# Fused AdaLN, linear attention and mixture of experts on one core: fewer TensorE signals, longer GELU and weight rings

## What is computed

```python
h = _layernorm(x, axis=-1) * (1 + ca) + sa
x = x + ga * _L0_attn_ref(h, ...)      # 8 heads of 16
h = _layernorm(x, axis=-1) * (1 + cb) + sb
x = x + gb * _L0_ffn_ref(h, ...)       # 8 experts of 256, 2 per token
```

```python
num = jnp.einsum('bshd,bhde->bshe', q, kv) * scale + vsum[:, None, :, :]
den = jnp.einsum('bshd,bhd->bsh', q, ksum) * scale + seq_len
o = num / den[..., None] + lepe_conv(v, lepe_w, lepe_b)   # 5 taps along the tokens
o = o.reshape(Bb, Ss, H * DV) * o_gate
return o @ Wo.T
```

```python
h = jax.nn.gelu(jnp.einsum('bsd,edh->besh', x, W1) + b1[None, :, None, :], approximate=False)
out = jnp.einsum('besh,ehd->besd', h, W2) + b2[None, :, None, :]
y = jnp.einsum('bse,besd->bsd', gates, out)
```

## Time and profile before

| what | value |
|---|---|
| median of 3 runs | 488.49 us (486.08 to 492.94) |
| the profiled execution's own time | 489.41 us |
| its span, first to last instruction | 487.5 us |
| busy: PE, PEld | 408.9 us (84%), 341.1 us (70%) |
| busy: DVE, ACT, POOL | 329.3, 297.4, 299.1 us |
| mean granted TensorE clock | 0.934 of full speed |
| DMA moved | 107.81 MB, 221 GB/s on average |
| chain that ended last | PE 58%, POOL 11%, DMA 10%, DVE 7%, ACT 6% |

### The profile page before, as it was taken

How to read it: one execution, slowest core, us unless ns; L and a number is a source line. 1 busy time by engine, 2 the same in 40 slices (tenths; PEclk the granted TensorE clock), 3 DMA queues, 4 the chain that set the end, 5 groups by cost and what they waited for, 6 DMA issues and landing times.

```text
span 487.5 us, 9883 instructions
## 1 busy us (share of the span) xinstructions
PE 408.9 (84%) x2808; PEld 341.1 (70%) x2808; DVE 329.3 (68%) x1070; ACT 297.4 (61%) x805; POOL 299.1 (61%) x293
## 2 busy tenths in 40 slices
PE   2578787599999999999999999999988969688410
PEld 2355374288899879887988798879877857587200
DVE  3297987897787588988988898778864710333342
ACT  1454553488679687868786878587566644465200
POOL 0320127717623787878787877777787777737671
PEclk9998876999999999999999998999999997899755
DMA  7920501489988798888998897779889998999521
GB/s 238 298 79 2 167 2 43 129 238 282 280 248 250 226 269 253 260 235 266 273 262 236 266 300 225 233 218 309 244 254 283 283 319 245 266 289 312 153 74 39
DMA packets 113845, 107.81 MB, mean 221 GB/s; under 512 B 10040, under 2 KB 85440, under 8 KB 113536
## 3 DMA queue, kind: packets, MB, share of 16 engines
q1 hardware_dynamic: 80848, 77.76, 54.8%
q0 software_dynamic: 8192, 16.79, 11.3%
q10 hardware_dynamic: 24752, 12.64, 8.6%
HBM read 76.47 MB, written 30.68 MB: 220 GB/s over the span
## 4 chain that ended last, share of the span: by engine, by line
PE 58%; POOL 11%; DMA 10%; DVE 7%; ACT 6%; issue 6%; SPq 1%; POOLq 0%; ACTq 0%; DVEq 0%
PE ps_hid L451 13%; PE ps_o L462 12%; PE bank L347 6%; POOL x_sort L637 5%; POOL og L647 4%; PE ps_x L439 3%; DMA o_sort<-o_s 3%; ACT xn L489 3%; PE bank L360 3%; PE ps_z L470 3%; PE bank L415 2%; DMA og<-o_sort,slots 2%; PE bank L381 2%; PE bank L391 2%; PE bank L375 2%
## 5 line engine op out<-in xcount | busy, mean ns | idle before, releaser
L637 POOL DMA_INDIRECT x_sort<-xn,slots x128 | 138.1, 1079 | 65.0 <-issue 36.6
L647 POOL DMA_INDIRECT og<-o_sort,slots x128 | 126.6, 989 | 48.1 <-issue 44.4
L574 ACT ACTIVATE hid<-ps_hid,wbuf 128x128 f32<-128x128 f32 x368 | 104.5, 374 | 33.0 <-PE ps_hid L451 27.2
L451 PE MATMUL ps_hid<-xs_t,wbuf 128*128 128x128 f32 x736 | 101.6, 282 | 7.4 <-DMA wbuf<-in_w_all 4.3
L462 PE MATMUL ps_o<-wbuf,hid 128*128 128x128 f32 x736 | 99.3, 283 | 4.9 <-ACT hid L574 3.9
L451 PEld LDWEIGHTS ps_hid<-xs_t,wbuf 128*128 128x128 f32 x736 | 92.6, 195 | 13.4 <-issue 5.6
L462 PEld LDWEIGHTS ps_o<-wbuf,hid 128*128 128x128 f32 x736 | 91.2, 196 | 13.4 <-issue 6.6
L833 DVE SCALAR_TENSOR_TENSOR u<-og,gate,ps_z 128x128 f32<-128x128 f32 x64 | 22.0, 343 | 72.8 <-DMA og<-o_sort,slots 47.4
L613 POOL TENSOR_TENSOR rstd<-var_eps,minus_half 128x8 f32<-128x8 f32 x16 | 27.2, 1700 | 61.8 <-DVE var_eps L668 61.6
L347 PE MATMUL bank<-wqkvg_f,h 128*128 128x384 f32 x128 | 51.4, 527 | 7.5 <-ACT v L514 6.5
L564 ACT ACTIVATE xs_t<-ps_x,mod 128x512 f32<-128x512 f32 (+1 forms) x48 | 37.3, 777 | 18.1 <-PE ps_x L439 17.9
(11 more groups left out here) (122 smaller groups left out, 629.1 us busy)
## 6 DMA issues: line engine op xcount, KB each, us to landing
wbuf<-in_w_all SPq DMA_DIRECT2D x184, 257.0 KB, 3.6
xg<-x_sort SPq DMA_DIRECT2D x40, 256.0 KB
o_sort<-o_s ACTq DMA_DIRECT2D x40, 256.0 KB
x_sort<-zero SPq DMA_DIRECT2D x20, 256.0 KB, 4.4
xs<-in_x SPq DMA_DIRECT2D x8, 512.0 KB, 5.6
out<-y SPq DMA_DIRECT2D x16, 256.0 KB
x_sort<-xn,slots POOLq DMA_INDIRECT x128
og<-o_sort,slots POOLq DMA_INDIRECT x128, 4.3
```

Of the source, the lines that this page charges most:

```text
L451: last = pe.matmul(ps_hid[k % 2][:, m % 2, h, :], wbuf[w % W_RING][:, h * P:(h + 1) * P], xs_t[g % XS_RING][:, t], start=True, stop=True)
L574: last = act.activation(hid[k % HID_RING][:, m % 2, h, :], ps_hid[k % 2][:, m % 2, h, :], ACT.Gelu, bias=w[:, 2 * HID + h:2 * HID + h + 1])
L637: pool.indirect_dma_start(x_sort[b % SORTS], bass.IndirectOffsetOnAxis(ap=at, axis=0), xn2[i][:, n, :], None).then_inc(s_scat[b % SORTS], 16)
L647: pool.indirect_dma_start(og[:, k, n, :], None, o_sort[i], bass.IndirectOffsetOnAxis(ap=at, axis=0)).then_inc(s_gat[n], 16)
```

## The change

It touches three kinds of signal and two ring sizes. No instruction that computes or moves data is added, taken away or moved on any engine; what changes is which instruction raises a semaphore, and what number is waited for.

- q, k, v: TensorE raises `s_qkv` once per pair of tiles instead of once per tile. VectorE waits for the pair before it rotates its first tile.
- The transposes of v and of q: `s_vT` and `s_qT` are raised once, after both halves, instead of once for each half. ScalarE waits for both before it evacuates the first.
- Second products: `s_l2` is raised after each second pair and after the last of a batch, so once per group of up to four tiles, 6 instead of 12 per batch. The three waits for it are changed to match: weights (L288), GELU buffer (L574), output copy (L582).
- `HID_RING` goes from 2 to 4 and `W_RING` from 8 to 10. The weights of tile k now wait for the whole group that tile k - 10 was in.

```diff
-        W_RING, XG_RING, XS_RING, HID_RING, O_RING = 8, 3, 2, 2, 2
+        W_RING, XG_RING, XS_RING, HID_RING, O_RING = 10, 3, 2, 4, 2
...
                     if k >= W_RING:
                         old_b, old_t = divmod(k - W_RING, TILES)
-                        sp.wait_ge(s_l2, couple(old_b, old_t // 2) + 1)
+                        sp.wait_ge(s_l2, group(old_b, old_t // GROUP) + 1)
...
                     for j in (2 * n, 2 * n + 1):
                         t = slice(j * P, (j + 1) * P)
                         bank_free(f"qkv_{j}", b)
-                        pe.matmul(of(f"qkv_{j}", b)[:, 0:3 * D], h1[i][:, t], wqkvg_f[:, 0:3 * D], start=True, stop=True)\
-                            .then_inc(s_qkv, 1)
+                        last = pe.matmul(of(f"qkv_{j}", b)[:, 0:3 * D], h1[i][:, t], wqkvg_f[:, 0:3 * D], start=True, stop=True)
+                    last.then_inc(s_qkv, 1)
...
                         for j in range(JC):
                             last = pe.transpose(of(f"vT_{c}", b)[:, j * P:(j + 1) * P], v[:, c * JC + j, 0:D], ident)
-                        last.then_inc(s_vT, 1)
+                    last.then_inc(s_vT, 1)
...
                         for j in range(JC):
                             last = pe.transpose(of(f"qT_{c}", b)[:, j * P:(j + 1) * P], qk[:, c * JC + j, 0:D], ident)
-                        last.then_inc(s_qT, 1)
+                    last.then_inc(s_qT, 1)
...
-                    last.then_inc(s_l2, 1)
+                    if n % 2 or n == PAIRS - 1:
+                        last.then_inc(s_l2, 1)
...
                     for c in range(CH):
-                        act.wait_ge(s_vT, CH * b + c + 1)
+                        act.wait_ge(s_vT, b + 1)
...
                     for c in range(CH):
-                        act.wait_ge(s_qT, CH * b + c + 1)
+                        act.wait_ge(s_qT, b + 1)
...
                     if k >= HID_RING:
-                        act.wait_ge(s_l2, k - HID_RING + 1)
+                        act.wait_ge(s_l2, (k - HID_RING) // 2 + 1)
...
-                    act.wait_ge(s_l2, couple(b, min(PAIRS, (n + 1) * GROUP // 2)))
+                    act.wait_ge(s_l2, group(b, n) + 1)
...
                     for j in (2 * n, 2 * n + 1):
-                        dve.wait_ge(s_qkv, J * b + j + 1)
+                        dve.wait_ge(s_qkv, J // 2 * b + j // 2 + 1)
```

## The result

The changed kernel takes **497.81 us** (median of 4 runs, 497.71 to 498.96) against 489.91 us of the kernel before (4 runs, 486.08 to 492.94): a ratio of 1.0166, 95% interval 1.0121 to 1.0211. The forecast was 492.7 us, range 488.5 to 497.0: the time lies 0.8 us above the range, and the loss is 7.9 us where the sum said 4.2. The profiled execution took 497.71 us (span 495.8, mean granted clock 0.93).

A forecast was written before the change was run, and what follows sets the result against it. TensorE bounds the middle (120 to 360 us), an engine-to-engine chain the head. Terms 2.65 + 2.3 + 0.25 + 0 + 0 - 1.0 = +4.2 us on the median 488.49 give 492.7 us, range 488.5 to 497.0.

The forecast's parts named there:

- Head, +2.65: Batches 0 to 2: rotation starts 0.04 us after the pair's second matmul; delays of 0.75, 0.95 and 0.95 us.
- Middle, +2.3: Batches 3 to 7: late copies of v free a PSUM bank late; TensorE waits 0.4 or 0.5 us per batch.
- Transposes, +0.25: Batch 2: ScalarE's evacuation starts 0.38 us late, freeing L360's bank about 0.25 us late; other batches 0, upper bound 3.8.
- Signals and GELU ring, 0: 96 fewer increments change nothing; nothing needs the GELU sooner after its 3.5 us wait near the end: 0 for both.
- Weight ring, -1.0: Tail after 418 us: about half of the first products' 2.0 us of weight waits goes; bounds 0 and -2.0 or -3.
- Absorbed (489.4): Rival, chance 0.27: middle stalls are made up, GpSimd's scatter hides part of the head's delays, the tail gains: 489.4 us.
- The ring pays (488): Rival, chance 0.10: load-limited tail gains 3 us as removed stalls keep the clock up; head and middle costs halve: 488.
- Signals cost: Rival, chance 0.05: each increment holds TensorE 26 ns, so fewer of them save 2.5 us: 490.2 us.
- Slower by over 2%: Rival, chance 0.07: in batches 3 to 7 all four pairs reach TensorE through a late GELU, 13 us: 503.4 us.

The follow-up runs named there:

- e5: The kernel before with the q, k, v pair signal only in batches 0 to 2: 495.47 against 491.74 us, ratio 1.0068.
- e6: The kernel before with the q, k, v pair signal only in batches 3 to 7: 493.58 us, ratio 1.0045.
- e1: The kernel before with the q, k, v pair signal alone, in all batches: 499.06 against 491.84 us, ratio 1.0115.
- e2: The kernel before with only the single signal for both halves of the transposes of v and q: 492.07 against 491.84 us, ratio 0.9991.
- e13: The changed kernel measured again on an ordinary chip, beside the kernel before: 500.44 against 493.70 us, ratio 1.0161.
- e14: The kernel before with the pair signal and the single transpose signal, rings as before: 500.25 against 493.70 us, ratio 1.0157.
- e15: The kernel before with the pair signal and the rings with their coarser release, transposes as before: 498.96 us, ratio 1.0127.
- e7: The kernel before with 544 more increments of spare semaphores on first and second products: 490.91 against 491.74 us, ratio 0.9986.
- e3: The kernel before with only the rings (weights ten, GELU four) and one second-product signal per four tiles: 491.39 against 491.84 us, ratio 0.9986.
- e4: The changed kernel with the signal per q, k, v tile restored: 490.08 us against 491.84 of the kernel before, ratio 0.9965.
- the fillers: Useless matmuls in TensorE's gaps in batches 0 to 2: kernel before 497.78 us, changed kernel 500.25, changed kernel without pair signal 495.65.
- e12: The changed kernel with the signal per q, k, v tile restored, as e4, on a slow chip: 658.42 us, ratio 1.0056 to the kernel before.
- e11: The changed kernel measured again on a slow chip: 661.58 us against 655.68 of the kernel before, ratio 1.0153.

## Why the prediction was right or wrong

**Head, +2.65: right in place and about right in size.** The rotation starts behind the second matmul, 0.04 us after it (58.82 against 58.78). e5, which has this term alone, measures +3.3 us (1.2 to 5.5). By batch e5's matmuls are late by 0.74, then 2.07 more (2.81 - 0.74), then 0.75 more (3.56 - 2.81), where I had 0.75, 0.95, 0.95; but e6, without an edit in the head, is as late at the start of batch 1 (+0.93), and e1, with it, is not (+0.09). So single profiles do not confirm the split by batch, and where 0.74 and 0.75 fit, it can be luck. The start of the expert work, expected some 3 us later, came 6.3 us later in the changed kernel and 3.6 to 3.8 in e5 and e1.

**Middle, +2.3: right.** The shift in batches 3 to 7 is 0.55 + 0.57 + 0.29 + 0.27 + 0.56 = 2.24 us, with 0.5 expected in three batches and 0.4 in two, through the engine and the banks that were named. e6 measures +2.2 (0.5 to 4.0). A batch passes on less than one pair's 0.65 us, so the slower rival (every pair through a late GELU) is excluded. But it comes at two places, 0.20 us by the third pair and 0.36 at the last in batch 4, where I had the last alone: the weights at 180.07 in the earlier trace rows are the last pair's.

**Transposes, +0.25: right alone, too small beside the pairs.** e2 shows -0.4 (-2.1 to +1.3), which excludes the upper bound of 3.8 for the transposes alone. Beside the pairs they cost 1.5 to 2.5 us (e13 and e14 against e15). I had priced each edit against the kernel before and added them up.

**Signals and GELU ring, 0: right.** For the first, e7, which excludes anything over 1.0 us for 544 increments. For the second, the wait of 3.5 us of the GELU for ps_o near the end has no row in the changed kernel, and e3 gains nothing that can be measured.

**Weight ring, -1.0: not seen in the changed kernel** (e3 leaves it open, e13 against e14 shows none). The first products' waits for weights near the end were 2.0 us in three places; now (stretch 426 to 463 us, the same work):

```profile
PE ps_hid L451 <- DMA wbuf<-in_w_all: 2.8, 4, 1.2
```

The longest, 1.23, stands at 450.88. The mistake was to price a wait at the place of the old one. The queue waits less at that line, but more at the next. Waits of SyncE's queue in the changed kernel:

```profile
SPq L288 <- PE ps_o L462: 55.2, 27, 5.8
...
SPq L298 <- DMA x_sort<-xn,slots: 28.6, 8, 7.9
SPq L298 <- PE ps_x L439: 21.9, 14, 6.6
```

At L288 it waits 55.2 us instead of 91.1. At L298, where the same queue issues the loads of the sorted rows, it waits 28.6 and 21.9 us instead of 7.9 and 7.1, and the next weights stand behind that. The sum of the three is 105.7 us, and was 106.1: the wait has moved and not gone. DMA moves 285 GB/s from 418 to 455 us, 292 before.

**The steps that failed are in the sum.** The costs of the pairs held. The sum adds them, and the other delays, to 488.49 us as if each stood alone. Three things are wrong with it: the base, the clock, which it puts at nothing without a reason, and the transposes beside the pairs.

*The base.* The median 488.49 came from three runs, and their spread of 6.9 us was used for what can be told apart, but not for the base. The mean of 81 later runs of the kernel before is 491.5 us, and that of each of the four jobs lies between 491.1 and 491.9. From there 4.2 would have given 495.7, inside the range and 2.1 below what was measured. That the number left the range is for the most part this; that the loss is 7.9 and not 4.2 us is not, as e13 shows.

*The clock.* Each run comes with its mean granted clock. Over these 81 runs time and clock go together with a correlation of -0.70: 2.3 us for each 0.01 (2.1 to 2.8 by job), around 0.931. Kernels with the pairs in all batches have a lower mean clock: 0.9253 (the changed kernel), 0.9238 (e13), 0.9248 (e14), 0.9255 (e15), 0.9268 (e1). That is 0.004 to 0.007 lower, or 1.0 to 1.6 us that no term holds. Taken at equal clock, in us over the kernel before (standard errors 0.4 to 0.7):

```
changed  e13   e14   e15   e1    e5 head  e6 middle  e2    e3     e4    e7
 +5.2   +7.2  +7.3  +5.1  +4.9   +2.9      +2.5     +0.8  -0.9   -0.8  -0.8
```

e5 and e6 fall on the forecast's 2.65 and 2.3, and e1 and e15 on their sum. e7, which should be at 0, shows how far such a number can be trusted. The correction is an estimate: the runs do not show whether the edits lower the clock or whether a longer wait, which costs time by itself, also shows as a lower mean clock. In the trace of the changed kernel, TensorE was idle longer from 20 to 105 us (62.75 busy us of 85 instead of 66.16), its clock was low from 95.3 us for 13.7 us, and the kernel lost 5.7 us from the start of batch 2 to the first expert product (6.29 - 0.57). The pairs without the transposes (e1, e5, e15) lose 0.5 to 0.8 us there, at a clock of 1.00, so this loss is not the pairs' alone. And from 20 to 105 us the lowest clock of all, 0.80, is in e6's profile, which has no edit there. That an edit causes the lower clock is therefore argued and not shown; the fillers, which were to show it, moved more than the clock.

*The transposes beside the pairs*, as above: +0.25 in the sum, 1.5 to 2.5 us by e13, e14 and e15, and by the table 2.1 to 2.4 us at equal clock (7.2 - 5.1, 7.3 - 4.9). How the two edits act on each other stays open.

So of the 5.4 us between the forecast of 492.7 and the mean of the first four runs, 498.1, 3.1 are the base, 1.3 the clock (0.0057 lower, at 2.3 us for 0.01) and 1.0 the delays at equal clock (5.2 against 4.2). The ten runs of both measurements have a mean of 499.4, 7.9 us over 491.5: some 1.5 clock and 6.4 delays, of which the pairs' own are about 5 and the rest goes with the transposes.

**The rivals.** Absorbed (489.4): false, the shift of the middle is not made up. The ring pays (488): false in the changed kernel; its largest support is e4, 1.8 us faster than before, which e12 does not repeat. Signals cost: false by e7. Slower by over 2%: its mechanism is false, though the measured ratio does not exclude the size.

## What to carry to other kernels

A signal for two tiles instead of one delays an in-order consumer by the gap between the two (0.65 us here), and the loss arrives wherever that consumer frees a PSUM bank: here two rows of the timeline gave it to a tenth of a us, also under a saturated TensorE. Increments on TensorE cost nothing that could be measured, so a signal is to be merged only where its consumer is not waiting. Two edits that cost 5.7 us and nothing alone cost some 2 us more together (e13 to e15): such costs are not simply added. A forecast of a per cent needs a base from more than three runs.

## What the runs showed of the hardware

- The same kernel takes 488.3 us at a mean granted clock of 0.935 and 494.6 at 0.924 (the kernel before, two of the 17 runs beside e13); over all its runs on ordinary chips it ranges from 486.1 to 500.3 us. Where the clock drops differs from one execution to the next, and one short drop costs some 1.6 us in the stretch where TensorE never waits (e1's clock is low for 3.4 us from 208.2 us, and its matmuls fall 1.64 us further behind between batch 4, +5.04, and batch 5, +6.68).
- 544 more increments on matmuls of 111 ns a record cost nothing that can be measured (0.9951 to 1.0021).
- One chip ran three kernels (the one before, e11, e12) in some 644 to 671 us, at a mean clock of 0.80 to 0.84, with VectorE and ScalarE busy as long as elsewhere (e11).
